# Second cross attention: two heads of attention at once, with probabilities and values split into high and low parts

## Chip, cores and metric

One core of a Trainium2 chip runs the whole program. The metric is the device time of one execution in microseconds (us).

## The reference, cut to what matters

The input is x of 8 batches of 256 rows by 256 columns, with a context of 64 rows for each batch. Two gated layers follow each other: a cross attention, a self attention with a mixture of experts, a second cross attention, a feed-forward block. The change lies in the second cross attention. Of each batch it computes, with 16 query heads of width 128 and 4 key/value heads (4 query heads share one):

```
q = rope(rms_norm(h @ wq));  k = rope(rms_norm(h @ wk));  v = h @ wv
kc = rms_norm(ctx @ wk_ctx); vc = ctx @ wv_ctx
p = softmax(q @ [kc, k].T / sqrt(128) + causal mask on the k part)   # 64 + 256 keys
x = x + tanh(g_xattn) * ((p @ [vc, v]) @ wo)
```

All of it is asked for in float32.

## The kernel before

The second cross attention is `cross_attention_1`. It walks over 32 items, NI = 4 groups x 8 batches. Item i is key/value head g = i // 8 of batch i % 8 with its four query heads h = 0 to 3. Rows are tiled in T = 2 tiles of 128. Each engine runs an order of its own that is written out by hand for one item, and engines meet only at counting semaphores. In an item's body j = i + 1 and k = i + 2 are the items of which earlier steps are already done: projections for k, transposes and first scores for j. The steps, by engine:

- TensorE (`pe`): `proj_kv`, `proj_q` (into the two banks of pA), `q_tr`, `k_tr`, `p_tr` (transposes of queries, keys and probabilities, into the two banks of pT in turn), `scores` (pS, two banks), `attend` (probabilities times values, into the one bank pO), `out_proj` (pF). Projections and `out_proj` go through `three` (L458 to L462), three matmuls of fp32r operands (high x high, high x low, low x high). `scores` and `attend` are plain float32 matmuls; the profile shows each as two instructions.
- ScalarE (`act`): `take_kv` (squares of k, copy of v), `squares` (of q), `exp`, `normalise` (the scaling by 1/sum, two instructions), the copies out of pT (`q_ev`, `k_ev`, `p_ev`), `o_ev` (the high part of pO), `w_high`.
- VectorE (`dve`): `soft` (mask and maximum, from pS), `recip`, `take_q` (two products of rope, from pA), `rotate_k`, `o_low` (the low part of pO, pO minus the high part), `add_out` (L1555, into the residual).
- GpSimd (`pool`): sums of rope, inverse norms, `context_values` (values of the context, laid on the upper or the lower half of the partitions), `context_keys`, `w_low`.

`attend(i, h)` of one head waits for the copy of the transposed probabilities (`te`) and, as pO has one bank, for `o_low` of the head before (`ot`):

```
e.matmul(pO[:, 0:S], V[:, i % 3, 0, :], PT[:, h % 2, P:P + S], start=True, stop=False)
e.matmul(pO[:, P:S], V[:, i % 3, 1, :], PT[:, h % 2, P + S:2 * P + S], start=False, stop=False)
for t in range(T):
    ins = e.matmul(pO[:, t * P:(t + 1) * P], VS[:, i % 2, t, :], PT[:, h % 2, 0:P],
                   start=False, stop=(t == 1))
```

Of the kernel before, what the change touches and what calls it, by code (L numbers as in the profile page):

```python
# [24 lines left out]
P = 128  # L25
# [42 lines left out]
def build(nc, d, out, spill, stop=99):  # L68
    ctx = ExitStack()
    with ctx:  # L70
# [1109 lines left out]
        def cross_attention_1(scope, KT, VC, w_here, cw_here, w_next, cw_next):  # L1180
# [24 lines left out]
            V = sb(name + "_V", [P, 3, T, HD], F32, scope)  # L1205
            VS = sb(name + "_VS", [P, 2, T, HD], F32, scope)
# [5 lines left out]
            PT = sb(name + "_PT", [P, 2, 4 * P], F32, scope)  # L1212
# [4 lines left out]
                     "const", "table", "vz", "vs")  # L1217
            q = {x: sem(f"{name}_{x}") for x in names}
            raw_in = [q["raw0"], q["raw1"]]

            def at_qk(i, n):

                return n if i == 0 else NT + PER * (i - 1) + (2, 3, 5)[n]

            def at_p(i, h):
                return NT + PER * i + (h if i == NI - 1 else (0, 1, 4, 6)[h])
# [25 lines left out]
            def pe(e):  # L1252
# [27 lines left out]
                def q_tr(i, t):  # L1280
                    c = at_qk(i, t)
                    e.wait_ge(q["te"], pos(c - 1))
                    e.wait_ge(q["rope"], NT * i + 2 + t)
                    for h in range(HG):
                        ins = e.transpose(pT[:, c % 2, h * P:(h + 1) * P], QR[:, t, h * HD:(h + 1) * HD],
                                          ident[:, :])
                    ins.then_inc(q["tr"], 1)

                def k_tr(i):
                    c = at_qk(i, 2)  # L1290
                    e.wait_ge(q["te"], pos(c - 1))
# [13 lines left out]
                def p_tr(i, h):  # L1305
                    c = at_p(i, h)
                    e.wait_ge(q["pn"], HG * i + h + 1)
                    e.wait_ge(q["te"], pos(c - 1))
                    for j, b in enumerate((1, 0, 3, 2)):
                        ins = e.transpose(pT[:, c % 2, j * P:(j + 1) * P], PB[:, h, b * P:(b + 1) * P],  # L1310
                                          ident[:, :])
                    ins.then_inc(q["tr"], 1)

                def attend(i, h):
                    e.wait_ge(q["te"], at_p(i, h) + 1)
                    e.wait_ge(q["ot"], HG * i + h)
                    if h == 0:
                        e.wait_ge(q["kv"], i + 1)
                        e.wait_ge(q["vs"], i + 1)
                    e.matmul(pO[:, 0:S], V[:, i % 3, 0, :], PT[:, h % 2, P:P + S], start=True, stop=False)  # L1320
                    e.matmul(pO[:, P:S], V[:, i % 3, 1, :], PT[:, h % 2, P + S:2 * P + S], start=False, stop=False)
                    for t in range(T):
                        ins = e.matmul(pO[:, t * P:(t + 1) * P], VS[:, i % 2, t, :], PT[:, h % 2, 0:P],
                                       start=False, stop=(t == 1))
                    ins.then_inc(q["pv"], 1)

                def out_proj(i, t):
                    g = i // 8
                    e.wait_ge(q["ot"], HG * i + HG)
                    e.wait_ge(q["split"], 8 * g)  # L1330
                    e.wait_ge(q["acc"], i)
                    r = slice(t * P, (t + 1) * P)
                    for h in range(HG):
                        cc = slice(WO + h * D, WO + (h + 1) * D)
                        ins = three(e, pF[:, t * D:(t + 1) * D], OTh[:, i % 2, h, r], OTl[:, i % 2, h, r],
                                    Wh[(g + 1) % 2][:, cc], Wl[(g + 1) % 2][:, cc], h == 0, h == HG - 1)
                    if t == T - 1:
                        ins.then_inc(q["f"], 1)
# [12 lines left out]
                for i in range(NI):  # L1351
# [20 lines left out]
                    attend(i, 2)  # L1372
# [9 lines left out]
                    attend(i, 3)  # L1382
# [4 lines left out]
            def act(e):  # L1387
                def take_kv(i):
                    e.wait_ge(q["proj"], NU * i + 1)
                    e.wait_ge(q["pv"], pos(HG * (i - 2)))  # L1390
                    x = pA[:, NU * i % 2, :].rearrange("p (t a n) -> p t a n", t=T, a=2)
                    for t in range(T):
                        e.activation(sk[:, t, :], x[:, t, 0, :], ACT.Square, accum_out=ssk[:, t:t + 1])
                    e.activation(V[:, i % 3, :, :], x[:, :, 1, :], ACT.Copy).then_inc(q["kv"], 1)
# [66 lines left out]
                for i in range(NI):  # L1461
# [30 lines left out]
                    o_ev(i, 3)  # L1492
                    if two:
                        squares(k, 1)
                phase_end(e, name)

            def dve(e):
# [70 lines left out]
                for i in range(NI):  # L1568
                    j, k = i + 1, i + 2
                    one, two = j < NI, k < NI  # L1570
                    soft(i, 2)
                    recip(i, 2)
                    o_low(i, 0)
# [19 lines left out]
                    o_low(i, 3)  # L1593
# [3 lines left out]
            def pool(e):  # L1597
# [678 lines left out]
```

## Time and profile before

| | |
|---|---|
| median of 3 runs | 1992.56 us (1992.42 to 1993.39) |
| profiled execution | 1994.94 us, of which span 1993.1 us |
| TensorE busy in the span | 1786.4 us (90%) |
| ScalarE | 1305.8 us (66%) |
| VectorE | 1086.7 us (55%) |
| GpSimd | 1072.5 us (54%) |

A span runs from the first to the last instruction of the core. Busy shares are averages over stages with different limits, so they don't say what the second cross attention waits for; that is read from its own stretch, about 1262 us to 1852 us of the span. In a timeline row "x4" means that four instructions are merged; the duration then reaches from the start of the first to the end of the last. An instruction's duration includes its way through the pipeline, so the next one of the same engine starts a little before it ends. The distance from start to start is called pitch in this document.

### The profile page before, as it was taken

The page shows a single profiled execution, that of the slowest core. Times are in us where ns is not written, and L with a number is a line of the kernel's source. Part 1 is how long each engine was busy: PE and PEld are TensorE (multiplying, and loading weights), DVE is VectorE, ACT ScalarE, POOL GpSimd, SP SyncE. Part 2 cuts the span into 40 slices and gives each one's busy share as a digit, 9 for nine tenths or more (in the row PEclk, how much of TensorE's full clock was granted, in tenths as well). Part 3 has the DMA queues.
Part 4 walks back from the last instruction along what each step waited for, and adds up shares of the span by engine and source line. Part 5 has one row for each costly group of instructions (what it writes and reads, how often), then busy time and mean ns, then how long its engine had stood idle before and what let it go on. Part 6 is the DMA issues. An engine that isn't in the chain of part 4 may idle for free. (4 is left out here: it accounts for less than half of the span.)

```text
span 1993.1 us, 36721 instructions
## 1 busy us (share of the span) xinstructions
PE 1786.4 (90%) x11712; PEld 1603.9 (80%) x11712; DVE 1086.7 (55%) x3117; ACT 1305.8 (66%) x4189; POOL 1072.5 (54%) x1187
## 2 busy tenths in 40 slices
PE   3499999269999999999988985799999999999698
PEld 1388888259999999999877863688888888888598
DVE  1477777656666666666534434455555555555422
ACT  1277777158888888888723313688888888888221
POOL 1433334389988988898730103544544454453364
PEclk9699999679999999999968986899999999999799
DMA  3000001110000000000001110000000000000000
GB/s 108 22 17 17 17 23 33 45 32 17 18 22 17 15 19 17 17 17 12 12 1 32 30 41 11 16 11 11 8 11 11 8 11 14 18 14 13 4 22 22
DMA packets 28385, 40.25 MB, mean 20 GB/s; under 512 B 4770, under 2 KB 18338, under 8 KB 27940
## 3 DMA queue, kind: packets, MB, share of 16 engines
q1 hardware_dynamic: 28196, 37.90, 6.3%
q8 instruction: 98, 1.61, 0.3%
q14 instruction: 91, 0.75, 0.1%
HBM read 33.69 MB, written 4.19 MB: 19 GB/s over the span
## 5 line engine op out<-in xcount | busy, mean ns | idle before, releaser
L460 PE MATMUL pA<-Wh,XTh 128*128 128x512 f32 (+1 forms) x512 | 222.6, 435 | 8.4 <-DVE x_tk L1524 3.8
L1163 POOL TENSOR_TENSOR f_sw<-f_sw,f_sin 128x512 f32<-128x512 f32 x128 | 183.6, 1434 | 38.7 <-ACT f_sw L969 38.7
L462 PE MATMUL pA<-Wh,XTl 128*128 128x512 f32 (+1 forms) x512 | 190.1, 371 | 0.0
L461 PE MATMUL pA<-Wl,XTh 128*128 128x512 f32 (+1 forms) x512 | 189.7, 370 | 0.0
L969 ACT ACTIVATE f_sw<-pA 64x512 f32<-64x512 f32 x256 | 151.8, 593 | 36.6 <-PE pA L875 32.8
L873 PE MATMUL pA<-XTh,Wh 128*128 128x256 f32 x512 | 163.7, 320 | 8.4 <-POOLq L116 6.2
L1166 POOL TENSOR_TENSOR f_sw<-f_sw,f_RB 128x512 f32<-128x512 f32 x128 | 165.1, 1290 | 10.0
L455 POOL TENSOR_TENSOR Wl<-RAW,Wh 128x256 fp32r<-128x256 f32 (+3 forms) x64 | 60.9, 952 | 175.0 <-ACT Wh L448 175.0
L1427 ACT ACTIVATE x_P<-x_P,x_nm 128x192 f32<-128x192 f32 (+1 forms) x256 | 128.0, 506 | 33.7 <-DVE x_nm L1536 33.7
L875 PE MATMUL pA<-XTh,Wl 128*128 128x256 f32 x512 | 145.9, 285 | 0.0
L874 PE MATMUL pA<-XTl,Wh 128*128 128x256 f32 x512 | 145.9, 285 | 0.0
L1631 POOL TENSOR_TENSOR x_QR<-x_QR,x_t 128x512 f32<-128x512 f32 x64 | 82.1, 1283 | 99.4 <-DVE x_QR L1513 99.4
L990 ACT ACTIVATE f_P<-f_P,f_nm 128x128 f32<-128x128 f32 (+1 forms) x256 | 114.1, 447 | 16.6 <-DVE f_nm L1076 16.5
L460 PEld LDWEIGHTS pA<-Wh,XTh 128*128 128x128 f32 x512 | 98.5, 192 | 29.3 <-DVE x_tk L1524 4.3
L1435 ACT ACTIVATE x_P<-x_P,x_rs 128x192 f32<-128x192 f32 (+1 forms) x256 | 116.3, 508 | 8.4 <-DVE x_rs L1544 8.4
L299 PE MATMUL pT<-ident,n_xn 128*128 128x128 f32 x160 | 44.1, 432 | 84.3 <-DVE n_xn L260 83.9
L1536 DVE CUSTOM_DVE_ANT_0 x_P<-pS,x_mask,x_nrq 128x192 f32<-128x192 f32 (+1 forms) x256 | 113.6, 481 | 3.5 <-PE pS L1302 2.7
L461 PEld LDWEIGHTS pA<-Wl,XTh 128*128 128x128 f32 x512 | 98.8, 193 | 18.7
L462 PEld LDWEIGHTS pA<-Wh,XTl 128*128 128x128 f32 x512 | 98.7, 193 | 17.0
L873 PEld LDWEIGHTS pA<-XTh,Wh 128*128 128x128 f32 x512 | 98.8, 193 | 11.4 <-POOLq L116 6.6
L299 PEld LDWEIGHTS pT<-ident,n_xn 128*128 128x128 f32 x160 | 29.9, 224 | 97.0 <-issue 51.5
L1076 DVE CUSTOM_DVE_ANT_0 f_P<-pS,f_mask 128x128 f32<-128x128 f32 (+1 forms) x256 | 80.8, 353 | 45.7 <-PE pS L882 45.6
(245 smaller groups left out, 6276.8 us busy)
## 6 DMA issues: line engine op xcount, KB each, us to landing
RAW<-in_w_f SPq DMA_DIRECT2D x32, 256.0 KB, 2.7
RAW<-in_w_x SPq DMA_DIRECT2D x32, 160.0 KB, 2.2
RAW<-in_w_x SPq DMA_DIRECT2D x32, 128.0 KB, 2.0
RAW<-in_w_ff SPq DMA_DIRECT2D x8, 288.0 KB, 2.8
R<-in_x SPq DMA_DIRECT2D x4, 512.0 KB, 5.8
x_spill<-R SPq DMA_DIRECT2D x1, 2048.0 KB, 7.5
RAW<-in_w_moe SPq DMA_DIRECT2D x8, 256.0 KB, 2.6
moe_xs<-x_spill SPq DMA_DIRECT2D x8, 256.0 KB, 3.0
```

The lines of the kernel that those rows point to most:

```text
L460: e.matmul(o, ah, bh, start=first, stop=False)
L461: e.matmul(o, ah, bl, start=False, stop=False)
L462: return e.matmul(o, al, bh, start=False, stop=last)
L873: e.matmul(o, Wh[g % 2][:, w], xh, start=(k == 0), stop=False)
L874: e.matmul(o, Wh[g % 2][:, w], xl, start=False, stop=False)
L875: ins = e.matmul(o, Wl[g % 2][:, w], xh, start=False, stop=(k == KD - 1))
L969: ins = e.activation(sw[dst, n, :, :], pA[src, n % 2, :].rearrange("p (a n) -> p a n", a=2), ACT.Copy)
L990: ins = e.activation(x, x, ACT.Exp, scale=-1.0, bias=nm[:, h, t:t + 1], accum_out=sm[:, h, t:t + 1])
L1163: e.tensor_tensor(y, y, bc(sind[:, :], 1, 2), ALU.mult).then_inc(q["swm"], 1)
L1166: e.tensor_tensor(y, y, RB[:, g % 2, 2 * n:2 * n + 2, :], ALU.add).then_inc(q["swb"], 1)
L1427: ins = e.activation(x, x, ACT.Exp, scale=-1.0, bias=nm[:, h, t:t + 1], accum_out=sm[:, h, t:t + 1])
L1435: ins = e.activation(x, x, ACT.Copy, scale=rs[:, h, t:t + 1])
```

## The change

`attend` takes two heads at a time: `attend(i, 0)` for heads 0 and 1, `attend(i, 1)` for heads 2 and 3, each over the whole bank pO (512 columns). It goes through `three`, with probabilities PTh/PTl and values Vh/Vl (own) and VSh/VSl (context) in fp32r. VectorE makes the low parts: `p_low` once a head from pT, `v_low` once an item from pA. GpSimd splits the context's values in `context_values`. A bank of pT that holds probabilities is free only when `p_low` is done (`bank_free`, `pl`). `o_ev` and `o_low` run twice an item over 512 columns instead of four times over 256. The orders of TensorE, ScalarE and VectorE are written anew.

```diff
@@ -1202,28 +1202,49 @@
...
-V = sb(name + "_V", [P, 3, T, HD], F32, scope)
-VS = sb(name + "_VS", [P, 2, T, HD], F32, scope)
+Vh = sb(name + "_Vh", [P, 3, T, HD], F32R, scope)
+Vl = sb(name + "_Vl", [P, 3, T, HD], F32R, scope)
+vu = sb(name + "_vu", [P, T, HD], F32, scope)
...
-PT = sb(name + "_PT", [P, 2, 4 * P], F32, scope)
+used = 8 * cw_here
+PTh, PTl = (w[0][:, used:used + 8 * P].rearrange("p (j h n) -> p j h n", j=4, h=2) for w in (Wh, Wl))
+VSh, VSl = (w[0][:, used + 8 * P:used + 12 * P].rearrange("p (u t n) -> p u t n", u=2, t=T)
+            for w in (Wh, Wl))
 OTh = sb(name + "_OTh", [P, 2, HG, S], F32R, scope)
 OTl = sb(name + "_OTl", [P, 2, HG, S], F32R, scope)
...
+turns = [("q", 0, 0), ("q", 0, 1), ("q", 0, 2)]
+for i in range(NI):
+    j = [i + 1] * (i + 1 < NI)
+    turns += [("p", i, 0), ("p", i, 1)] + [("q", x, n) for x in j for n in (0, 1)] + [("p", i, 2)]
+    turns += [("q", x, 2) for x in j] + [("p", i, 3)]
+place = {x: c for c, x in enumerate(turns)}
...
+def bank_free(e, c):
+
+
+    if c >= 2:
+        x = turns[c - 2]
+        if x[0] == "p":
+            e.wait_ge(q["pl"], HG * x[1] + x[2] + 1)
+        else:
+            e.wait_ge(q["te"], c - 1)
...
     def q_tr(i, t):
         c = at_qk(i, t)
-        e.wait_ge(q["te"], pos(c - 1))
+        bank_free(e, c)
...
@@ -1305,28 +1326,31 @@
...
-    def attend(i, h):
-        e.wait_ge(q["te"], at_p(i, h) + 1)
-        e.wait_ge(q["ot"], HG * i + h)
-        if h == 0:
+    def attend(i, w):
+        e.wait_ge(q["pl"], HG * i + 2 * w + 2)
+        e.wait_ge(q["ot"], 2 * i + w)
+        if w == 0:
             e.wait_ge(q["kv"], i + 1)
+            e.wait_ge(q["tk"], i + 1)
             e.wait_ge(q["vs"], i + 1)
-        e.matmul(pO[:, 0:S], V[:, i % 3, 0, :], PT[:, h % 2, P:P + S], start=True, stop=False)
-        e.matmul(pO[:, P:S], V[:, i % 3, 1, :], PT[:, h % 2, P + S:2 * P + S], start=False, stop=False)
-        for t in range(T):
-            ins = e.matmul(pO[:, t * P:(t + 1) * P], VS[:, i % 2, t, :], PT[:, h % 2, 0:P],
-                           start=False, stop=(t == 1))
+        v, c = i % 3, i % 2
+        three(e, pO[:, :], Vh[:, v, 0, :], Vl[:, v, 0, :], PTh[:, 1:3, :, :], PTl[:, 1:3, :, :], True, False)
+        three(e, pO[:, S:2 * S], Vh[:, v, 1, :], Vl[:, v, 1, :], PTh[:, 3, :, :], PTl[:, 3, :, :],
+              False, False)
+        for t in range(T):
+            ins = three(e, pO[:, t * S:(t + 1) * S], VSh[:, c, t, :], VSl[:, c, t, :],
+                        PTh[:, 0, :, :], PTl[:, 0, :, :], False, t == T - 1)
         ins.then_inc(q["pv"], 1)

     def out_proj(i, t):
         g = i // 8
-        e.wait_ge(q["ot"], HG * i + HG)
+        e.wait_ge(q["ot"], 2 * i + 2)
         e.wait_ge(q["split"], 8 * g)
         e.wait_ge(q["acc"], i)
...
@@ -1355,21 +1379,20 @@
         scores(i, 2)
         if two:
             proj_kv(k)
-        attend(i, 0)
         p_tr(i, 1)
         scores(i, 3)
         if one:
             q_tr(j, 0)
-            q_tr(j, 1)
         if i:
             out_proj(i - 1, 0)
-        attend(i, 1)
+        if one:
+            q_tr(j, 1)
+        attend(i, 0)
         p_tr(i, 2)
         if one:
             k_tr(j)
         if i:
             out_proj(i - 1, 1)
-        attend(i, 2)
         if one:
             scores(j, 0)
         if two:
@@ -1379,7 +1402,7 @@
             scores(j, 1)
         if two:
             proj_q(k, 1)
-        attend(i, 3)
+        attend(i, 1)
     for t in range(T):
         out_proj(NI - 1, t)
     phase_end(e, name)
...
@@ -1417,8 +1440,9 @@
     def p_ev(i, h):
         c = at_p(i, h)
         e.wait_ge(q["tr"], c + 1)
-        e.wait_ge(q["pv"], pos(HG * i + h - 1))
-        e.activation(PT[:, h % 2, :], pT[:, c % 2, :], ACT.Copy).then_inc(q["te"], 1)
+        e.wait_ge(q["pv"], 2 * i + h // 2)
+        e.activation(PTh[:, :, h % 2, :], pT[:, c % 2, :].rearrange("p (j n) -> p j n", j=4), ACT.Copy
+                     ).then_inc(q["te"], 1)
...
-    def o_ev(i, h):
-        e.wait_ge(q["pv"], HG * i + h + 1)
+    def o_ev(i, w):
+        e.wait_ge(q["pv"], 2 * i + w + 1)
         e.wait_ge(q["f"], pos(i - 1))
-        e.activation(OTh[:, i % 2, h, :], pO[:, 0:S], ACT.Copy).then_inc(q["oth"], 1)
+        e.activation(OTh[:, i % 2, 2 * w:2 * w + 2, :].rearrange("p h (t n) -> p t h n", t=T),
+                     pO[:, :].rearrange("p (t h n) -> p t h n", t=T, h=2), ACT.Copy
+                     ).then_inc(q["oth"], 1)
...
@@ -1466,32 +1492,30 @@
         exp(i, 2)
         if two:
             take_kv(k)
-        o_ev(i, 0)
         p_ev(i, 1)
         normalise(i, 2)
         if one:
             q_ev(j, 0)
+        exp(i, 3)
+        if one:
             q_ev(j, 1)
-        exp(i, 3)
-        o_ev(i, 1)
+        o_ev(i, 0)
         p_ev(i, 2)
         if one:
             k_ev(j)
         normalise(i, 3)
-        o_ev(i, 2)
         w_high(i)
         if one:
             exp(j, 0)
+            normalise(j, 0)
         p_ev(i, 3)
-        if one:
-            normalise(j, 0)
         if two:
             squares(k, 0)
         if one:
             exp(j, 1)
-        o_ev(i, 3)
         if two:
             squares(k, 1)
+        o_ev(i, 1)
...
@@ -1512,7 +1536,13 @@
...
+    def v_low(i):
+        e.wait_ge(q["kv"], i + 1)
+        x = pA[:, NU * i % 2, :].rearrange("p (t a n) -> p t a n", t=T, a=2)
+        e.tensor_tensor(Vl[:, i % 3, :, :], x[:, :, 1, :], Vh[:, i % 3, :, :].bitcast(F32), ALU.subtract)
+
     def rotate_k(i):
+        v_low(i)
         e.wait_ge(q["rk"], i + 1)
         if i >= 2:
...
@@ -1543,9 +1573,18 @@
...
+    def p_low(i, h):
+        c = at_p(i, h)
+        e.wait_ge(q["te"], c + 1)
+        e.tensor_tensor(PTl[:, :, h % 2, :], pT[:, c % 2, :].rearrange("p (j n) -> p j n", j=4),
+                        PTh[:, :, h % 2, :].bitcast(F32), ALU.subtract).then_inc(q["pl"], 1)
+
+    def o_low(i, w):
+        e.wait_ge(q["oth"], 2 * i + w + 1)
+        two_heads = slice(2 * w, 2 * w + 2)
+        e.tensor_tensor(OTl[:, i % 2, two_heads, :].rearrange("p h (t n) -> p t h n", t=T),
+                        pO[:, :].rearrange("p (t h n) -> p t h n", t=T, h=2),
+                        OTh[:, i % 2, two_heads, :].bitcast(F32).rearrange("p h (t n) -> p t h n", t=T),
                         ALU.subtract).then_inc(q["ot"], 1)
...
@@ -1569,28 +1608,30 @@
         j, k = i + 1, i + 2
         one, two = j < NI, k < NI
         soft(i, 2)
+        p_low(i, 0)
         recip(i, 2)
-        o_low(i, 0)
+        p_low(i, 1)
         soft(i, 3)
         if two:
             rotate_k(k)
         recip(i, 3)
-        o_low(i, 1)
+        o_low(i, 0)
         if i:
             add_out(i - 1)
-        o_low(i, 2)
+        p_low(i, 2)
         if one:
             soft(j, 0)
+            recip(j, 0)
         if two:
             take_q(k, 0)
-        if one:
-            recip(j, 0)
+        p_low(i, 3)
+        if one:
             soft(j, 1)
         if two:
             take_q(k, 1)
         if one:
             recip(j, 1)
-        o_low(i, 3)
+        o_low(i, 1)
...
@@ -1603,11 +1644,17 @@
...
     def context_values(i):
         g = i // 8
-        e.wait_ge(q["pv"], pos(HG * (i - 1)))
-        for t in range(T):
-            ins = e.tensor_scalar(VS[:, i % 2, t, :], VC[:, i % 8, g * HD:(g + 1) * HD],
-                                  half[:, t:t + 1], None, ALU.mult)
-        ins.then_inc(q["vs"], 1)
+        e.wait_ge(q["pv"], pos(2 * (i - 1)))
+        e.wait_ge(q["vs"], i)
+        for t in range(T):
+            ins = e.tensor_scalar(vu[:, t, :], VC[:, i % 8, g * HD:(g + 1) * HD], half[:, t:t + 1], None,
+                                  ALU.mult)
+        ins.then_inc(q["vu"], 1)
+        e.wait_ge(q["vu"], i + 1)
+        e.tensor_copy(VSh[:, i % 2], vu[:, :, :]).then_inc(q["vh"], 1)
+        e.wait_ge(q["vh"], i + 1)
+        e.tensor_tensor(VSl[:, i % 2], vu[:, :, :], VSh[:, i % 2].bitcast(F32), ALU.subtract
+                        ).then_inc(q["vs"], 1)
```

## Rows read from the trace of the kernel before

**Rows 1.** Windows; us, then busy us of each engine (instructions), granted clock, DMA.
```profile
1280.00:1840.00 560.00, 551.51 (x3709) 497.04 (x3710) 304.97 (x1008) 469.75 (x1734) 263.85 (x357) 1.00 0.04 12
1818.00:1852.00 34.00, 28.97 (x209) 25.96 (x207) 12.96 (x45) 23.75 (x75) 7.41 (x8) 1.00 0.00 1
```

**Rows 2.** Timeline of TensorE in one item: start us, duration us, line, tiles.
```profile
1568.17 0.66 PE L1285 MATMUL pT<-ident,x_QR 128*128 128x128 f32 x4 [0.20 <-ACT x_PT L1421]
...
1568.90 0.29 PE L462 MATMUL pF<-Wh,x_OTl 128*128 128x256 f32 x1
...
1570.09 0.59 PE L1320 MATMUL pO<-x_PT,x_V 128*128 128x256 f32 x2
...
1571.19 0.60 PE L1310 MATMUL pT<-ident,x_P 128*128 128x128 f32 x4
...
1573.27 0.59 PE L1320 MATMUL pO<-x_PT,x_V 128*128 128x256 f32 x2
...
1578.16 0.39 PE L461 MATMUL pA<-Wl,XTh 128*128 128x512 f32 x1
...
1579.32 0.59 PE L1320 MATMUL pO<-x_PT,x_V 128*128 128x256 f32 x2
```

**Rows 3.** Timeline of ScalarE in the same item, same columns.
```profile
1566.48 0.27 ACT L1393 ACTIVATE x_sk<-pA 128x128 f32<-128x128 f32 x1
...
1567.25 0.38 ACT L1441 ACTIVATE x_OTh<-pO 128x256 fp32r<-128x256 f32 x1
...
1576.36 0.46 ACT L1427 ACTIVATE x_P<-x_P,x_nm 128x192 f32<-128x192 f32 x1 [1.06 <-DVE x_nm L1536]
...
1577.27 0.19 ACT L1427 ACTIVATION_READ_ACCUMULATOR x_P<-x_P,x_nm 128x1 f32 x1
1577.36 0.58 ACT L1421 ACTIVATE x_PT<-pT 128x512 f32<-128x512 f32 x1
1578.22 0.91 ACT L1435 ACTIVATE x_P<-x_P,x_rs 128x192 f32<-128x192 f32 x2 [0.28 <-DVE x_rs L1544]
1579.03 0.26 ACT L1401 ACTIVATE pA<-pA 128x128 f32<-128x128 f32 x1
...
1579.88 0.26 ACT L1401 ACTIVATE pA<-pA 128x128 f32<-128x128 f32 x1
```

**Rows 4.** Timeline of VectorE in the same item, same columns.
```profile
1568.01 0.41 DVE L1536 CUSTOM_DVE_ANT_0 x_P<-pS,x_mask,x_nrq 128x192 f32<-128x192 f32 x1
...
1568.81 0.08 DVE L1536 DVE_READ_ACCUMULATOR2_ANT x_nm<- 128x1 f32 x1
1568.81 0.35 DVE L1522 SCALAR_TENSOR_TENSOR x_KR<-pA,x_ssk,x_cosk 128x128 f32<-128x128 f32 x1
...
1573.47 0.75 DVE L1555 SCALAR_TENSOR_TENSOR R<-pF,tanhg,R 128x512 f32<-128x512 f32 x1 [1.24 <-PE pF L462]
...
1576.83 0.69 DVE L1510 TENSOR_TENSOR x_t<-pA,x_sin 128x512 f32<-128x512 f32 x1 [0.50 <-PE pA L462]
...
1578.03 0.15 DVE L1544 RECIPROCAL x_rs<-x_sm 128x2 f32<-128x2 f32 x1
```

**Rows 5.** Line L266, a norm stage: durations in ns, least, median, most.
```profile
L266 DVE TENSOR_TENSOR XTl<-pT,XTh x24: 683/686/692, 67.9 to 1872.5; 128x512 fp32r<-128x512 f32 x24
```

**Rows 6.** Groups of the stage by line: busy us, mean ns of one.
```profile
L1626 POOL TENSOR_TENSOR x_KR<-x_KR,x_tk 128x256 f32<-128x256 f32 x31 | 22.6, 729 | 6.9 <-DVE x_tk L1524 3.2
```

**Rows 7.** Timeline of TensorE: items 0, 1 and 30.
```profile
1265.39 0.66 PE L1310 MATMUL pT<-ident,x_P 128*128 128x128 f32 x4 [1.94 <-ACT x_P L1435]
...
1271.21 1.19 PE L1320 MATMUL pO<-x_PT,x_V 128*128 128x256 f32 x2 [2.86 <-POOL x_VS L1608]
...
1287.37 0.60 PE L1310 MATMUL pT<-ident,x_P 128*128 128x128 f32 x4
...
1818.52 0.60 PE L1310 MATMUL pT<-ident,x_P 128*128 128x128 f32 x4
```

**Rows 8.** Line L1555, the residual add of each item: first and last start.
```profile
L1555 DVE SCALAR_TENSOR_TENSOR R<-pF,tanhg,R x32: 750/751/752, 1298.7 to 1851.6; 128x512 f32<-128x512 f32 x32
```

More of the change, by code:

```diff
@@ L1216, in cross_attention_1 @@
                      "rqb", "rq", "tr", "te", "sc", "sct", "ex", "rs", "pn", "pv", "oth", "ot", "f", "acc",
-                     "const", "table", "vz", "vs")
+                     "const", "table", "vz", "vs", "vu", "vh", "pl")
             q = {x: sem(f"{name}_{x}") for x in names}
             raw_in = [q["raw0"], q["raw1"]]
+            turns = [("q", 0, 0), ("q", 0, 1), ("q", 0, 2)]
[4 more added lines that the diff above has]
+            place = {x: c for c, x in enumerate(turns)}
             def at_qk(i, n):
-                return n if i == 0 else NT + PER * (i - 1) + (2, 3, 5)[n]
+                return place["q", i, n]
             def at_p(i, h):
-                return NT + PER * i + (h if i == NI - 1 else (0, 1, 4, 6)[h])
+                return place["p", i, h]
+            def bank_free(e, c):
[5 more added lines that the diff above has]
+                        e.wait_ge(q["te"], c - 1)
             def heads(x, swap=False):
@@ L1290, in k_tr @@
                     c = at_qk(i, 2)
-                    e.wait_ge(q["te"], pos(c - 1))
+                    bank_free(e, c)
                     e.wait_ge(q["rope"], NT * i + 1)
@@ L1307, in p_tr @@
                     e.wait_ge(q["pn"], HG * i + h + 1)
-                    e.wait_ge(q["te"], pos(c - 1))
+                    bank_free(e, c)
                     for j, b in enumerate((1, 0, 3, 2)):
@@ L1389, in take_kv @@
                     e.wait_ge(q["proj"], NU * i + 1)
-                    e.wait_ge(q["pv"], pos(HG * (i - 2)))
+                    e.wait_ge(q["pv"], pos(2 * (i - 2)))
                     x = pA[:, NU * i % 2, :].rearrange("p (t a n) -> p t a n", t=T, a=2)
@@ L1393, in take_kv @@
                         e.activation(sk[:, t, :], x[:, t, 0, :], ACT.Square, accum_out=ssk[:, t:t + 1])
-                    e.activation(V[:, i % 3, :, :], x[:, :, 1, :], ACT.Copy).then_inc(q["kv"], 1)
+                    e.activation(Vh[:, i % 3, :, :], x[:, :, 1, :], ACT.Copy).then_inc(q["kv"], 1)
                 def squares(i, t):
@@ L1544, in recip @@
                     e.reciprocal(rs[:, h, :], sm[:, h, :]).then_inc(q["rs"], 1)
-                def o_low(i, h):
-                    e.wait_ge(q["oth"], HG * i + h + 1)
-                    e.tensor_tensor(OTl[:, i % 2, h, :], pO[:, 0:S], OTh[:, i % 2, h, :].bitcast(F32),
+                def p_low(i, h):
[9 more added lines that the diff above has]
+                                    OTh[:, i % 2, two_heads, :].bitcast(F32).rearrange("p h (t n) -> p t h n", t=T),
                                     ALU.subtract).then_inc(q["ot"], 1)
```

## The prediction

> **What bounds the kernel now.** I read first the windows over the stretch of the second cross attention. From 1280 to 1840 us TensorE is busy for 551.51 of 560 us (98.5%) at the full granted clock (1.00, the 2.4 GHz level), ScalarE for 469.75 (84%), VectorE for 304.97 (54%), GpSimd for 263.85 (47%) [rows 1]. So one item after another is set by TensorE's work. The length of an item comes from the first transpose of probabilities (L1310) of item 1, at 1287.37, and of item 30, at 1818.52 [rows 7]: 531.15 us over 29 items, 18.32 us each, of which 1.5% or 0.28 us is idle and 18.04 us work. One of its waits is the second `q_tr`, 0.20 us, for the copy of probabilities out of pT [rows 2]. Then I read the timelines of one item for each engine, because the change touches all their orders: they give the price and the pitch of each step [rows 2 to 4].
>
> **TensorE's share of the change.** A head of `attend` now takes from 1570.09 to 1571.19, 1.10 us [rows 2], so four heads 4.40. The new one for two heads is three matmuls of 512 columns and nine of 256 (three for V's second half, six for the context's). A 512 in fp32r has a pitch of (1579.32 - 1578.16)/5 = 0.232 us, a 256 one of (1570.09 - 1568.90)/10 = 0.119 us [rows 2]. That makes 0.70 + 1.07 = 1.77 us for two heads, 3.54 an item, 0.86 less than now. TensorE would have 17.18 us of work an item.
>
> **The work that is added elsewhere.** `p_low` is a subtraction of 512 columns from PSUM with an fp32r output. L266 is the same instruction in another stage and takes 0.68 to 0.69 us [rows 5]; next to another such instruction the pitch is (1578.03 - 1576.83)/2 = 0.60 [rows 4]. Four of them add 2.4 us an item to VectorE, `v_low` less than one more (0 to 0.6), and `o_low`, twice at 0.60 instead of four shorter ones, at most 1.2. VectorE has 54% of 18.32, 10.0 us, now and would have up to 14.2 of about 18: as a load it is no bound. ScalarE keeps its 15.4 us: two copies of 512 for four of 256, no more than now. GpSimd adds a copy and a subtraction of 256 columns to `context_values`. The subtraction is like L1626, 0.73 us [rows 6]; the copy I bound by nothing and 0.73. At most 1.5 us on 8.6 of 18.3 us, and what it makes is wanted an item later, so it is hidden, except in item 0 (below). No transfer changes.
>
> **Why the load isn't the answer.** The new orders tie the engines in a ring. `attend(i, 0)` needs `p_low(i, 1)`; `p_low(i, 2)` stands behind `add_out(i - 1)`, which waits for `out_proj(i - 1, 1)`, which stands behind `attend(i, 0)` on TensorE. ScalarE now has `normalise(j, 0)` right behind `exp(j, 0)`, so it waits there for VectorE's `recip(j, 0)`, and `p_ev(i, 3)` stands behind both. `p_low(i, 3)` waits for that copy, `soft(j, 1)` and `take_q(k, 1)` stand behind `p_low(i, 3)`, `squares(k, 1)` waits for `take_q(k, 1)`, and `o_ev(i, 1)`, which was ahead of `squares(k, 1)`, is now last on ScalarE, behind it. `o_low(i, 1)` waits for `o_ev(i, 1)`, and the next item's `soft` of head 2 stands behind `o_low(i, 1)`. So the ring closes once an item. Round it, in us, a step's pitch where the next stands behind it on the same engine, its end plus the hand-off where another engine takes over:
>
> 1. `o_ev` of the item before 0.60 (`p_ev`, of the same size, takes 0.58), hand-off 0.04; `o_low` 0.60; `soft(i, 2)` (1568.89 - 1568.01) 0.88 + 0.04 [rows 3, 4]: 2.16.
> 2. `exp(i, 2)` 1.00, `take_kv` 0.77, `p_ev(i, 1)` 0.58 + 0.04 [rows 3]: 2.39, together 4.55.
> 3. `p_low(i, 1)` 0.69 [rows 5] + 0.04 to TensorE: 5.28.
> 4. `q_tr(j, 1)` (1568.90 less two pitches of 256, less 1568.17) 0.49, `attend(i, 0)` 1.77: 7.54.
> 5. `p_tr`, `k_tr`, `out_proj(i - 1, 1)`, from 1571.19 to 1573.27, and 0.20 to `add_out` [rows 2, 4]: 9.82.
> 6. `add_out` 0.67 (0.75 less the overlap of 0.08), `p_low(i, 2)` 0.60, `soft(j, 0)` 0.92: 12.01.
> 7. `exp(j, 0)` to the end of its sum (1576.36 to 1577.46) 1.10 + 0.04, `recip` to the start of `normalise` (1578.03 to 1578.22) 0.19, `normalise` (1578.22 to 1579.03) 0.81, `p_ev(i, 3)` 0.62 [rows 3, 4]: 14.77.
> 8. `p_low(i, 3)` 0.60, `soft(j, 1)` (1568.01 to 1568.81) 0.80, `take_q(k, 1)` 1.20 + 0.08 + 0.04: 17.49.
> 9. `squares(k, 1)`, four of (1579.88 - 1579.03)/3 = 0.283 [rows 3], 1.13: 18.62.
>
> I also followed the steps beside the ring with the same prices: TensorE reaches `p_tr(i, 1)` some 0.5 us before `normalise(i, 1)` is done, comes to `q_tr(j, 1)` 0.1 to 0.2 us before `p_low(i, 1)`, and to `attend(i, 1)` 0.9 us before `p_low(i, 3)`. These waits go into the 18.62 - 17.18 = 1.44 us that TensorE idles per item. The hand-off of 0.04 is read where ScalarE was waiting for VectorE: `recip` ends at 1578.18, `normalise` starts at 1578.22 [rows 3, 4].
>
> The page "Advanced Engine Details and Errata" of the Trainium skill (section Miscellaneous Facts, Network/Comms) gives 50 to 100 ns for reading a semaphore from a sequencer. By that figure as the price of each of the ring's ten hand-offs the ring would be 18.7 to 19.2 us instead of 18.62, 3 to 17 us more in all; the row above shows 0.04, so I don't take it.
>
> **The sum.** Items 1 to 29: 29 x (18.62 - 18.32) = +8.8 us. Item 0 takes 1287.37 - 1265.39 = 21.98 us now. In it TensorE idles 2.86 us at `attend(0, 0)` until the context's values come, and then runs at half its clock (two instructions of L1320 take 1.19 us against 0.59) [rows 2, 7]. After the change, `p_tr`, `scores` and the two `q_tr` go ahead of `attend(0, 0)`, which starts when the split values are there, 1.2 to 1.5 us later than now, at about 1272.6. From there to the end of the item the ring's steps give some 10.4 us: item 0 takes 17.6, -4.3 us. If the clock falls as before it is nearly 0. The last two items have no projections; now they take from 1818.52 to 1852.35 [rows 7, 8], 33.8 us. Item 30 walked without `take_kv`, `take_q` and `squares` comes to 18.4, item 31, where each head's copy, low part, attend and output follow each other with nothing beside them, to 17.8: +2.4 us (bounds +0.5 and +3.5). In all +8.8 - 4.3 + 2.4 = +6.9 us. The profiled execution (span 1993.1, time 1994.94) is 2.4 us above the median of the runs; its 1994.94 would become 2001.8, and the median of 1992.56 becomes 1999.5.
>
> **Bounds.** With every hand-off at nothing the ring is 18.2 us; with each full duration (0.69) for the 0.60 of low parts in it, 18.9. 29 items make that -3.5 to +17 us instead of +8.8. With the bounds of item 0 and the tail that is 1983 to 2017.
>
> **Rivals.**
> - *TensorE stays the bound (faster).* The waits overlap with work better than my ring says, and the item becomes 17.18 us of work plus the 0.28 idle of now, 17.46. Then 29 x 0.86 = 24.9, and 1992.6 - 24.9 - 1.9 gives 1966. For it: 98.5% busy TensorE, 16% idle ScalarE, 46% idle VectorE. Against: the ring would have to be 1.1 us shorter than I sum it, which is more than all its hand-offs. It decides once the ring is under 17.46. 12%. The page "FP8 and Floating Point Precision" (section Matmul Precision) of the Trainium skill states four passes for float32; as column passes two heads would go from 5120 to 3840. That is the rule by which this change gains; the rows give 2.20 to 1.77 us.
> - *No change that can be told.* The ring comes out between 18.2 and 18.45, and the item is as long as now: 1989 to 1996, about 1993. For it: my sum is only 0.30 us above today's item. 25%.
> - *The clock falls.* If TensorE's new pauses (0.5 and 0.9 us in an item) brought the half clock for a few us in each item, as the 2.86 us pause in item 0 does now [rows 7], work would be stretched by 2 to 3 us and cost 1 to 2 us an item beyond the idle time: 2030 to 2055. Against: from 1818 to 1852 TensorE is 15% idle at a granted clock of 1.00 [rows 1]. 5%.
> - *The ring as summed (my forecast).* 58%, with 1995 to 2010 as its own range.
>
> **Numbers.** I predict 1999.5. The range 1984 to 2010 holds my case and that of no change; it leaves out the faster rival (12%), the fallen clock (5%) and little of the tails. 0.2% or 4 us is about what a measurement of this kernel can tell from no change. Slower by more than that: my case less the part of it under 1996.5, 0.51, and the fallen clock, 0.05, so 0.56. Within it: most of the second rival and that part of mine, 0.27. Faster: the first rival and a ring under 18.1, 0.17.
>
> **What the profile after would show.** Right: L461/L462 of pO with pitch 0.119 and 0.232; 18.4 to 18.8 us from one L1310 of head 0 to the next; TensorE near 92% busy; `p_low` at 0.69 us; ScalarE idle before `normalise` of head 0 for VectorE's reciprocal; the copy of pO starting behind `squares`; TensorE waiting on `p_low` before `attend(i, 1)`. Wrong: a period under 18.2 with TensorE at 97% or more, a granted clock under 1.00, `p_low` far from 0.69, or item 0 still over 20 us.

## The result and the profile after

The changed kernel takes 2004.04 us (median of 5 runs, 2000.03 to 2006.59), the kernel before beside it 1993.39 us (1992.42 to 1996.10). The ratio is 1.0049, with a 95% interval of 1.0033 to 1.0065: slower, by 10.65 us in the medians. The profiled execution took 2005.44 us, with a span of 2003.6 us against 1993.1.

Windows over the stage, and over its last two items; columns as in [rows 1]:

```profile
1280.00:1840.00 560.00, 525.19 (x3403) 456.74 (x3402) 366.33 (x1078) 463.77 (x1647) 294.54 (x416) 1.00 0.04 12
1820.00:1862.00 42.00, 31.11 (x200) 26.68 (x199) 20.47 (x57) 25.48 (x77) 9.80 (x11) 0.96 0.00 1
```

TensorE is busy for 525.19 of 560 us where it was 551.51 [rows 1], at the same granted clock of 1.00. VectorE rose from 304.97 to 366.33, ScalarE fell a little. So TensorE got the time back and waits it away. The timeline of TensorE in one item shows where (in brackets: idle before, and what ended it):

```profile
1560.60 0.50 PE L460 MATMUL pO<-Wh,x_Vh 128*128 128x512 f32 x1 [0.78 <-DVE Wl L1579]
...
1565.62 0.66 PE L1331 MATMUL pT<-ident,x_P 128*128 128x128 f32 x4 [0.24 <-ACT x_P L1459]
...
1568.99 0.66 PE L1306 MATMUL pT<-ident,x_QR 128*128 128x128 f32 x4
1569.40 0.48 PE L460 MATMUL pO<-Wh,x_Vh 128*128 128x512 f32 x1
...
1571.26 0.60 PE L1331 MATMUL pT<-ident,x_P 128*128 128x128 f32 x4
...
1579.22 0.50 PE L460 MATMUL pO<-Wh,x_Vh 128*128 128x512 f32 x1 [0.78 <-DVE Wl L1579]
...
1581.10 0.60 PE L1331 MATMUL pT<-ident,x_P 128*128 128x128 f32 x4
```

An item is 1579.22 - 1560.60 = 18.62 us. The fp32r matmuls of `attend` take 1571.26 - 1569.40 = 1.86 us for two heads. From the first of them, behind the transposes, to the second it is 0.31 us (1569.40 to 1569.71), where the pitch is 0.23; the prediction had these 0.08 us in the term of `q_tr`. TensorE waits 0.78 us for the low part of the probabilities (L1579, `p_low`, whose output lies in tile Wl) before `attend(i, 1)`, and 0.24 us for ScalarE's `normalise` before `p_tr(i, 1)`.

VectorE in the same item. L1585 is `o_low`, L1579 `p_low`, L1542 `v_low`, L1574 `recip`:

```profile
1564.32 0.69 DVE L1585 TENSOR_TENSOR x_OTl<-pO,x_OTh 128x512 fp32r<-128x512 f32 x1 [1.64 <-ACT x_OTh L1465]
...
1568.24 0.69 DVE L1579 TENSOR_TENSOR Wl<-pT,Wh 128x512 fp32r<-128x512 f32 x1 [1.10 <-ACT Wh L1444]
...
1569.65 0.42 DVE L1542 TENSOR_TENSOR x_Vl<-pA,x_Vh 128x256 fp32r<-128x256 f32 x1
...
1573.53 0.75 DVE L1594 SCALAR_TENSOR_TENSOR R<-pF,tanhg,R 128x512 f32<-128x512 f32 x1 [0.76 <-PE pF L462]
1574.20 0.68 DVE L1579 TENSOR_TENSOR Wl<-pT,Wh 128x512 fp32r<-128x512 f32 x1
...
1576.85 0.17 DVE L1574 RECIPROCAL x_rs<-x_sm 128x2 f32<-128x2 f32 x1 [1.16 <-ACT x_P L1451]
...
1578.47 0.69 DVE L1579 TENSOR_TENSOR Wl<-pT,Wh 128x512 fp32r<-128x512 f32 x1 [0.25 <-ACT Wh L1444]
```

`p_low` takes 0.68 to 0.69 us. VectorE is idle for 1.64 us before `o_low` until the copy of pO is there, and for 1.16 us before the reciprocal of head 0. ScalarE shows the other side. L1424 is `squares`, L1465 `o_ev`, L1459 `normalise`, L1444 `p_ev`:

```profile
1563.42 0.26 ACT L1424 ACTIVATE pA<-pA 128x128 f32<-128x128 f32 x1
...
1563.70 0.58 ACT L1465 ACTIVATE x_OTh<-pO 128x512 fp32r<-128x512 f32 x1
...
1577.05 0.91 ACT L1459 ACTIVATE x_P<-x_P,x_rs 128x192 f32<-128x192 f32 x2 [0.23 <-DVE x_rs L1574]
1577.86 0.58 ACT L1444 ACTIVATE Wh<-pT 128x512 fp32r<-128x512 f32 x1
...
1582.32 0.58 ACT L1465 ACTIVATE x_OTh<-pO 128x512 fp32r<-128x512 f32 x1
```

The copy of pO starts at 1563.70, right behind the last of the squares, though the last matmul of `attend` had started before 1562.48. And `normalise` of head 0 waits for the reciprocal (0.23 us, [idle before]) and holds up `p_ev` of head 3. These are the ring's places.

The first and last items: TensorE's first transpose of items 0, 1, 30 and 31 (L1331), and the second `attend` of item 30; in the kernel before these are in [rows 7, 8]:

```profile
1265.19 0.66 PE L1331 MATMUL pT<-ident,x_P 128*128 128x128 f32 x4 [1.91 <-ACT x_P L1459]
...
1283.23 0.60 PE L1331 MATMUL pT<-ident,x_P 128*128 128x128 f32 x4
...
1823.12 0.60 PE L1331 MATMUL pT<-ident,x_P 128*128 128x128 f32 x4
...
1839.62 0.50 PE L460 MATMUL pO<-Wh,x_Vh 128*128 128x512 f32 x1 [2.69 <-DVE Wl L1579]
...
1842.64 1.02 PE L1331 MATMUL pT<-ident,x_P 128*128 128x128 f32 x4
```

The residual adds (L1594), as the group of that line:

```profile
L1594 DVE SCALAR_TENSOR_TENSOR R<-pF,tanhg,R x32: 750/751/752, 1294.3 to 1860.5; 128x512 f32<-128x512 f32 x32
```

By these rows the span's 10.5 us come from: the stage begins 0.20 us earlier; item 0 takes 18.04 us instead of 21.98, -3.94; items 1 to 29 take (1823.12 - 1283.23)/29 = 18.617 us instead of 18.316, +8.73; items 30 and 31 take 38.13 instead of 33.83, +4.30; all that follows takes 142.35 instead of 140.75, +1.60. The last is outside the change, whose edits all lie in the second cross attention. Of the feed-forward block's first matmuls, those of 256 columns take 0.41 us each at the half clock (1.2 GHz) until the clock rises. The kernel before comes first, then the changed one:

```profile
1873.27 0.58 PE L1968 MATMUL pA<-XTh,Wh 128*128 128x256 f32 x1 [1.46 <-DVEq L116]
...
1877.92 0.32 PE L1968 MATMUL pA<-XTh,Wh 128*128 128x256 f32 x1
```

```profile
1882.07 0.58 PE L2015 MATMUL pA<-XTh,Wh 128*128 128x256 f32 x1 [1.46 <-DVEq L116]
...
1887.14 0.41 PE L2017 MATMUL pA<-XTh,Wl 128*128 128x256 f32 x1
```

The clock rises 4.65 us after the first matmul in the one, and has not risen after 5.07 us in the other. The block's second group of matmuls starts 6.27 us after the first in the kernel before (1879.54) and 7.12 us after it in the changed one (1889.19). That is 0.85 of the 1.60 us; the rest lies further on and is not traced.

### The profile page after: what moved, and what is told of

Its sections match the earlier page's. It is cut to its first block and busy times, and to the rows that moved or that the text cites. A ratio compares the mean times of both kernels' runs of the same rounds, so it can differ in the third digit from the quotient of the medians.

```text
span 2003.6 us, 36210 instructions
## 1 busy us (share of the span) xinstructions
PE 1769.7 (88%) x11456; PEld 1571.4 (78%) x11456; DVE 1157.6 (58%) x3213; ACT 1308.2 (65%) x4125; POOL 1105.6 (55%) x1251
## 5 line engine op out<-in xcount | busy, mean ns | idle before, releaser
L1459 ACT ACTIVATE x_P<-x_P,x_rs 128x192 f32<-128x192 f32 (+1 forms) x256 | 116.5, 510 | 7.2 <-DVE x_rs L1574 7.2
L461 PEld LDWEIGHTS pA<-Wl,XTh 128*128 128x128 f32 x512 | 99.0, 193 | 18.6
L1579 DVE TENSOR_TENSOR Wl<-pT,Wh 128x512 fp32r<-128x512 f32 x128 | 88.0, 688 | 43.0 <-ACT Wh L1444 42.8
```

What stands on the lines that cost most here:

```text
L461: e.matmul(o, ah, bl, start=False, stop=False)
L1459: ins = e.activation(x, x, ACT.Copy, scale=rs[:, h, t:t + 1])
```

## The experiments

All are made from the changed kernel. Each was timed in turns with the kernel before. Runs of one kernel spread by up to 8.5 us, so the length of an item is the sharper measure. It is taken from two rows of the residual add, L1594 or the line it has in the run, some 25 items apart, both in items that have all their steps (the last ones lack projections and are shorter). In the changed kernel:

```profile
1331.51 0.75 DVE L1594 SCALAR_TENSOR_TENSOR R<-pF,tanhg,R 128x512 f32<-128x512 f32 x1 [0.75 <-PE pF L462]
...
1796.93 0.75 DVE L1594 SCALAR_TENSOR_TENSOR R<-pF,tanhg,R 128x512 f32<-128x512 f32 x1 [0.76 <-PE pF L462]
```

That is 465.42/25 = 18.617 us an item.

### The same work off TensorE, once on the ring and once beside it

```diff
+                    def product(o, ah, al, bh, bl, first, last):
+                        if w == 0:          # 1 in the other kernel
+                            return e.matmul(o, ah, bh, start=first, stop=last)
+                        return three(e, o, ah, al, bh, bl, first, last)
+
-                    three(e, pO[:, :], Vh[:, v, 0, :], Vl[:, v, 0, :], ...     # cut here
+                    product(pO[:, :], Vh[:, v, 0, :], Vl[:, v, 0, :], ...      # the other calls likewise
```

> The changed kernel, but attend(i, 0) alone makes only the product of the high parts (4 matmuls instead of 12, so the low parts of heads 0 and 1 are left out). It takes 1.18 us off TensorE in each item, on the ring: attend(i, 0) 0.59 instead of 1.77 us. Ring theory: the item becomes 18.62 - 1.18 = 17.44 us, in all about -34 us, some 1969. If TensorE's work were the bound: the same -34. If VectorE's added load or the clock were the cause: less than 10 us. Told apart from TensorE's work only beside the run that takes the same work off attend(i, 1).

> The same with attend(i, 1): only the product of the high parts for heads 2 and 3 (their low parts left out). TensorE has 1.18 us less work in each item here too, but attend(i, 1) is not on the ring: its end is followed by the copy of pO, which ScalarE reaches only behind squares(k, 1), 1.1 us or more later. Ring theory: item of 18.62 as before, 0 to -2 us in all, about 2002. TensorE's work as the bound: -34 us, about 1970.

Measured for `attend(i, 0)`: 2000.86 us against 1994.33 of the kernel before, ratio 1.0032 (1.0021 to 1.0043). The residual adds, and a row of TensorE:

```profile
1331.51 0.75 DVE L1599 SCALAR_TENSOR_TENSOR R<-pF,tanhg,R 128x512 f32<-128x512 f32 x1 [0.75 <-PE pF L462]
...
1809.48 0.75 DVE L1599 SCALAR_TENSOR_TENSOR R<-pF,tanhg,R 128x512 f32<-128x512 f32 x1 [0.75 <-PE pF L462]
...
1568.59 0.44 PE L1315 MATMUL pT<-ident,x_KR 128*128 128x128 f32 x2 [0.73 <-ACT x_qT L1436]
```

477.97/26 = 18.383 us an item: 0.23 less, not 1.18. This was a miss, and the last row shows where the rest went. `k_tr` (L1315) now waits 0.73 us for the copy of the second half of the queries, `q_ev(j, 1)` (L1436), which stands behind `exp(i, 3)` on ScalarE. The ring over `attend(i, 0)` had a second path beside it, only some 0.2 us shorter.

Measured for `attend(i, 1)`: 2005.47 us, ratio 1.0061 (1.0046 to 1.0076). The residual adds:

```profile
1331.94 0.75 DVE L1599 SCALAR_TENSOR_TENSOR R<-pF,tanhg,R 128x512 f32<-128x512 f32 x1 [0.75 <-PE pF L462]
...
1797.36 0.75 DVE L1599 SCALAR_TENSOR_TENSOR R<-pF,tanhg,R 128x512 f32<-128x512 f32 x1 [0.75 <-PE pF L462]
```

From the waits between 1300 and 1800 us, TensorE's for `normalise` (total us, times, longest):

```profile
PE pT L1331 <- ACT x_P L1464: 38.5, 27, 1.4
```

465.42/25 = 18.617 us an item, the same as with all the matmuls. `attend(i, 1)` took 0.69 us (1579.64 to 1580.33) instead of 1.88, and the 1.19 us became wait: 1.4 us before `p_tr(i, 1)` instead of 0.24. TensorE's work is not what sets the item.

### The same VectorE instruction, once on the ring and once where VectorE waits

```diff
+            junk = sb(name + "_junk", [P, 4 * P], F32, scope)
...
                     p_low(i, 3)
+                    e.tensor_tensor(junk[:, :], mask[:, :], mask[:, :], ALU.add)
                     if one:
                         soft(j, 1)
```

and in the other kernel the same line between `recip(j, 1)` and `o_low(i, 1)`.

> The changed kernel with one more VectorE instruction an item (mask + mask into a tile of its own, 512 columns, about 0.69 us long with a pitch of 0.60) between p_low(i, 3) and soft(j, 1), on the ring. Ring theory: 18.62 + 0.60 = 19.22 us an item, +17 to +20 us, about 2022. VectorE's load as the cause: the same as in the run with the instruction elsewhere. TensorE as the bound: no change.

> The same added instruction, but between recip(j, 1) and o_low(i, 1), where VectorE waits 1.64 us for the copy of pO. Ring theory: no change, 18.62 us an item, within 2 us of the changed kernel, about 2004. VectorE's load as the cause: +17 to +20 us, as with the instruction on the ring.

Measured on the ring: 2035.05 us, ratio 1.0206 (1.0190 to 1.0221). The residual adds; then GpSimd's sum of rope, the added instruction and the one behind it:

```profile
1336.56 0.75 DVE L1595 SCALAR_TENSOR_TENSOR R<-pF,tanhg,R 128x512 f32<-128x512 f32 x1 [0.75 <-PE pF L462]
...
1806.16 0.75 DVE L1595 SCALAR_TENSOR_TENSOR R<-pF,tanhg,R 128x512 f32<-128x512 f32 x1 [0.75 <-PE pF L462]
...
1576.12 1.26 POOL L1680 TENSOR_TENSOR x_QR<-x_QR,x_t 128x512 f32<-128x512 f32 x1 [3.38 <-DVE x_QR L1538]
...
1576.90 1.03 DVE L1629 TENSOR_TENSOR x_junk<-x_mask 128x512 f32<-128x512 f32 x1
1577.86 0.41 DVE L1567 CUSTOM_DVE_ANT_0 x_P<-pS,x_mask,x_nrq 128x192 f32<-128x192 f32 x1
```

469.60/24 = 19.567 us an item, 0.95 more, where 0.60 was expected. The instruction took 1.03 us instead of 0.67 in the next run and its pitch was 1577.86 - 1576.90 = 0.96. The ring carried exactly the pitch; the price of the instruction was wrong.

Measured beside the ring: 2007.30 us, ratio 1.0066 (1.0050 to 1.0083). The same rows; the added instruction starts first here, and GpSimd's takes 1.77 us instead of 1.26:

```profile
1332.91 0.75 DVE L1595 SCALAR_TENSOR_TENSOR R<-pF,tanhg,R 128x512 f32<-128x512 f32 x1 [0.75 <-PE pF L462]
...
1798.34 0.75 DVE L1595 SCALAR_TENSOR_TENSOR R<-pF,tanhg,R 128x512 f32<-128x512 f32 x1 [0.75 <-PE pF L462]
...
1564.00 0.67 DVE L1635 TENSOR_TENSOR x_junk<-x_mask 128x512 f32<-128x512 f32 x1
1565.72 0.69 DVE L1586 TENSOR_TENSOR x_OTl<-pO,x_OTh 128x512 fp32r<-128x512 f32 x1 [1.05 <-ACT x_OTh L1466]
...
1564.04 1.77 POOL L1680 TENSOR_TENSOR x_QR<-x_QR,x_t 128x512 f32<-128x512 f32 x1 [1.69 <-DVE x_QR L1538]
```

465.43/25 = 18.617 us an item, unchanged: VectorE's idle time before `o_low` took it up. The load of VectorE is not the cause.

### One part of the new order undone

```diff
                     if one:
                         exp(j, 0)
-                        normalise(j, 0)
                     p_ev(i, 3)
+                    if one:
+                        normalise(j, 0)
...
                         soft(j, 0)
-                        recip(j, 0)
                     if two:
                         take_q(k, 0)
+                    if one:
+                        recip(j, 0)
                     p_low(i, 3)
```

> The changed kernel with one part of its new orders undone: normalise(j, 0) again behind p_ev(i, 3) on ScalarE, recip(j, 0) again behind take_q(k, 0) on VectorE. It takes the wait for the reciprocal and the 0.81 us of normalise out of the ring, and take_q(k, 0) then covers exp(j, 0). Followed step by step: p_low(i, 3) starts 1.1 us earlier behind soft(j, 0), the item becomes about 17.55 us, -31 us in all, about 1973. If the loss came from the added low parts as such (VectorE's load): no change.

Measured: 1972.29 us against 1993.88 of the kernel before, ratio 0.9888 (0.9873 to 0.9903). The residual adds:

```profile
1330.20 0.75 DVE L1595 SCALAR_TENSOR_TENSOR R<-pF,tanhg,R 128x512 f32<-128x512 f32 x1 [0.76 <-PE pF L462]
...
1786.40 0.75 DVE L1595 SCALAR_TENSOR_TENSOR R<-pF,tanhg,R 128x512 f32<-128x512 f32 x1 [0.76 <-PE pF L462]
```

456.20/26 = 17.546 us an item, as followed (17.55). All the loss of an item, and 0.77 us more, hung on the place of one reciprocal and one scaling.

### The copy of pO ahead of the squares

```diff
                         exp(j, 1)
+                    o_ev(i, 1)
                     if two:
                         squares(k, 1)
-                    o_ev(i, 1)
```

> The changed kernel with o_ev(i, 1) ahead of squares(k, 1) on ScalarE, as it was before the change. The ring loses squares' 1.13 us there, but ScalarE still reaches normalise(i, 1) no earlier, so the path over p_tr(i, 1), scores(i, 3), q_tr(j, 0) and out_proj(i - 1, 0) takes over 0.2 us below: item 18.45, about -5 us, 1999. If only the ring counted: item 17.5, -33 us.

Measured: 2003.33 us, ratio 1.0048 (1.0031 to 1.0065). The residual adds, and TensorE's `p_tr(i, 1)` and `q_tr(j, 1)`:

```profile
1335.28 0.75 DVE L1594 SCALAR_TENSOR_TENSOR R<-pF,tanhg,R 128x512 f32<-128x512 f32 x1 [0.75 <-PE pF L462]
...
1798.34 0.75 DVE L1594 SCALAR_TENSOR_TENSOR R<-pF,tanhg,R 128x512 f32<-128x512 f32 x1 [0.76 <-PE pF L462]
...
1568.36 0.66 PE L1331 MATMUL pT<-ident,x_P 128*128 128x128 f32 x4 [0.36 <-ACT x_P L1459]
...
1571.58 0.60 PE L1306 MATMUL pT<-ident,x_QR 128*128 128x128 f32 x4
```

463.06/25 = 18.522 us an item, 0.095 less (0.17 expected). `q_tr(j, 1)` no longer waits; `p_tr(i, 1)` waits 0.36 us for `normalise`. That fits the path behind it being the longest now, as expected; no run shortens that path by itself to show it. Over 29 items 0.095 us make 2.8 us, which the run times can't show: the median is 0.7 us under 2004.04, and its four runs lie between 1999.64 and 2007.00. The profiled one is the slowest of them and reached the stage's first transpose 4 us later than the changed kernel (1269.24 against 1265.19), outside the change.

### Both paths over the first two heads shortened

```diff
                         q_ev(j, 0)
-                    exp(i, 3)
-                    if one:
                         q_ev(j, 1)
+                    exp(i, 3)
                     o_ev(i, 0)
```

together with the high parts alone in `attend(i, 0)`.

> As the run with only the high parts in attend(i, 0) (low parts of heads 0 and 1 left out), and q_ev(j, 1) ahead of exp(i, 3) on ScalarE. That run gained 0.24 us an item instead of 1.18, as k_tr then waited for q_ev(j, 1). With this second path shortened too, the 1.18 us must come out: item about 17.5 us, about -32 us against the changed kernel, 1972. If something else held the item at 18.4, it stays at 18.4, 2000.

Measured: 1974.78 us, ratio 0.9894 (0.9875 to 0.9913). The residual adds:

```profile
1344.45 0.74 DVE L1598 SCALAR_TENSOR_TENSOR R<-pF,tanhg,R 128x512 f32<-128x512 f32 x1
...
1782.99 0.74 DVE L1598 SCALAR_TENSOR_TENSOR R<-pF,tanhg,R 128x512 f32<-128x512 f32 x1
```

438.54/25 = 17.542 us an item (17.5 expected). That is 0.84 us less than with the high parts alone, once the copy of the queries stands ahead of `exp(i, 3)`. It fits the second path having held that run; the copy's move by itself was not run, and it also delays `exp(i, 3)` and `o_ev(i, 0)`.

### The whole computation in another order

```diff
                     normalise(i, 1)
+                    if i and one:
+                        squares(j, 1)
                     exp(i, 2)
...
-                    if two:
-                        squares(k, 1)
                     o_ev(i, 1)
...
+                    p_low(i, 2)
                     if i:
                         add_out(i - 1)
-                    p_low(i, 2)
```

with `normalise(j, 0)` and `recip(j, 0)` placed as in the run above.

> The whole computation of the changed kernel in another order: normalise(j, 0) and recip(j, 0) back as in the first run, o_ev(i, 1) last, squares(j, 1) behind normalise(i, 1) of the next item, p_low(i, 2) ahead of add_out(i - 1). Followed step by step, only a wait of 0.3 us at q_tr(j, 1) is left beside TensorE's 17.0 to 17.2 us of work: item about 17.3 us, about 1965, 1.4% faster than the kernel before. If the split itself costs more than it gives, it is not faster than the kernel before (1994).

Measured: 1964.62 us against 1993.88, ratio 0.9848 (0.9834 to 0.9863). The residual adds, and below them the window between these two:

```profile
1328.45 0.75 DVE L1595 SCALAR_TENSOR_TENSOR R<-pF,tanhg,R 128x512 f32<-128x512 f32 x1 [0.16 <-PE pF L462]
...
1777.91 0.75 DVE L1595 SCALAR_TENSOR_TENSOR R<-pF,tanhg,R 128x512 f32<-128x512 f32 x1 [0.16 <-PE pF L462]
```

```profile
1328.45:1777.91 449.46, 445.21 (x2966) 400.15 (x2965) 321.47 (x937) 396.52 (x1432) 257.23 (x364) 1.00 0.05 13
```

449.46/26 = 17.287 us an item (17.3 expected), with TensorE busy for 99.1% of it. It beats both kernels, the one before by 1.5%: the split pays once TensorE is kept fed. The single moves of this order were not run one by one, beyond the reciprocal and the scaling above.

## Why the prediction was right, point by point

- **TensorE's work.** 1.77 us for two heads was forecast from pitches of 0.232 and 0.119 us; from its start to the next transposes 1.86 was measured. With the 0.41 of `q_tr` before it that is 2.27 for step 4 of the ring, where 2.26 stood. In the last experiment, where TensorE sets the item, it is busy for 445.21/26 = 17.12 us of it, against the 17.18 of work in the prediction. In the changed kernel it is busy for 93.8%, where 92% stood: the waits of 0.78 and 0.24 us come to less than the 1.44 us of idle time forecast, and the first matmul behind a wait takes 0.34 us to the next instead of 0.23, which counts as busy.
- **Added work.** `p_low` 0.688 us against 0.69, `v_low` 0.42 within 0 to 0.6. The loads are no bound: shown by the VectorE instruction that cost nothing beside the ring.
- **The ring.** 18.62 us was summed and 18.617 measured, and not by luck of the sum: the starts in the changed kernel's timelines give each of the nine steps within 0.02 us.

| step | from | to | summed | measured |
|---|---|---|---|---|
| 1 | copy of pO, 1563.70 | `exp(i, 2)`, 1565.85 | 2.16 | 2.15 |
| 2 | `exp(i, 2)` | `p_low(i, 1)`, 1568.24 | 2.39 | 2.39 |
| 3 | `p_low(i, 1)` | `q_tr(j, 1)`, 1568.99 | 0.73 | 0.75 |
| 4 | `q_tr(j, 1)` | `p_tr(i, 2)`, 1571.26 | 2.26 | 2.27 |
| 5 | `p_tr(i, 2)` | `add_out`, 1573.53 | 2.28 | 2.27 |
| 6 | `add_out` | `exp(j, 0)`, 1575.72 | 2.19 | 2.19 |
| 7 | `exp(j, 0)` | `p_low(i, 3)`, 1578.47 | 2.76 | 2.75 |
| 8 | `p_low(i, 3)` | `squares(k, 1)`, 1581.20 | 2.72 | 2.73 |
| 9 | `squares(k, 1)` | copy of pO, 1582.32 | 1.13 | 1.12 |

  That the time hangs on the ring is shown by experiment at two of its places: the pitch of an instruction added behind `p_low(i, 3)` came out in full (0.95 for 0.96 us), and the place of `normalise(j, 0)` and `recip(j, 0)` was worth the 1.07 us that the walk gave. The same instruction and the same TensorE work off the ring were worth nothing. That TensorE idles before `attend(i, 1)` was forecast with 0.9 us and measured with 0.78, before `p_tr(i, 1)` 0.5 against 0.24.
- **What the ring's sum did not say.** It gives the length, but not what shortening one step is worth. The prediction noted the steps beside it, TensorE's path over `p_tr(i, 1)` included, but not the path over `q_ev(j, 1)` and `k_tr`, 0.2 us shorter than the ring. Taking 1.18 us out of `attend(i, 0)` gave 0.23. The expectation of that run was wrong for this reason.
- **Item 0.** -3.94 us against the forecast -4.3, at the full clock as assumed (granted clock 1.00 from 1265 to 1283). `attend(0, 0)` started at 1272.28, where 1272.6 stood, and from there to the end of the item it took 10.95 us, where 10.4 stood.
- **The tail.** This is the term that was mis-sized: +4.30 us against +2.4, outside its upper bound of 3.5. Right behind 2.69 us of idle time before the second `attend` of item 30 TensorE's clock fell to the half (1.2 GHz) for some 3 us: the granted clock is 1.00 from 1836 to 1840, 0.63 from 1839 to 1843 and 1.00 again from 1846 on. This `attend` takes 1842.64 - 1839.62 = 3.02 us instead of the 1.88 of full clock (1579.22 to 1581.10), and the copy of pO waits for it. That is 1.14 of the 1.9 us missed, and all that item 30 takes over its forecast: 19.52 us (1823.12 to 1842.64) against 18.4. Item 31 takes 18.6 us (to 1861.25) against 17.8; its first four transposes still run at the half clock (0.85 us to the next instruction instead of 0.43), and which of its steps holds the rest is open. The prediction weighed the clock for pauses below 1 us and for item 0, and not for the last items.
- **The rest.** +1.60 us lies behind the stage and was in no term. The instructions there are the same in both kernels; 0.85 us of it come with the clock that rises later in the feed-forward block. From the end of the last residual add to the end of the span the eight experiments above took 141.8 to 144.1 us, the changed kernel 142.35 and the one profiled execution of the kernel before 140.75. Whether this term follows from the change or from the chance of single executions is not shown.
- **The rivals.** TensorE as the bound is excluded by the run with less TensorE work off the ring, no change by an item of 18.617 us instead of 18.2 to 18.45 and by the interval of the ratio, the fallen clock by the granted 1.00 from 1280 to 1840 us. A hand-off took 0.04 us from ScalarE to VectorE (`o_ev` ends at 1564.28, `o_low` starts at 1564.32) and 0.06 from VectorE to TensorE (`p_low` ends at 1579.16, the matmul starts at 1579.22). The Trainium skill's page "Advanced Engine Details and Errata" (section Miscellaneous Facts) gives 50 to 100 ns for reading a semaphore; the first of these hand-offs lies under that, the second inside it, and the ring of 18.617 us leaves no room for it as the price of all ten.
- **The bounds.** The stated 1983 to 2017 doesn't come out of the terms given with it: 1992.56 - 3.5 - 4.3 + 0.5 is 1985.3, and 1992.56 + 17 + 0 + 3.5 is 2013.1. The forecast doesn't rest on it.
- In all: forecast +6.9 us, measured +10.65, interval of the ratio +6.6 to +13 us. Of the difference the ring's 29 items have next to nothing (+8.73 for +8.8); it lies in the tail, the rest and item 0.

## What to carry to other kernels

When four engines each run a fixed order, busy shares and saved work don't give the time: write down which step waits for which, follow the loop that returns to its start one item later, and sum pitches and hand-offs round it. Then look for the second-longest path before pricing any saving: here one took over after 0.2 us, another after 0.1. A quick step that answers another engine (a reciprocal, a copy that frees a bank) should stand where its input is just ready, not right behind its source and not behind a long step that nobody waits for. In this kernel the first was worth 1.07 us an item, the second by itself 0.095.

## What the runs showed of the hardware

- A VectorE instruction with both inputs in SBUF and a GpSimd instruction delay each other. On the ring GpSimd's sum (1576.12 to 1577.38) was under way when the added instruction started at 1576.90, and that took 1.03 us instead of 0.67. Beside the ring the added instruction started first, at 1564.00, and GpSimd's sum took 1.77 us instead of 1.26. The page "SBUF — State Buffer" of the Trainium skill (section SBUF: two separate sides) states such an exclusive lock of a shared port pair for a VectorE instruction with two SBUF inputs against a GpSimd instruction that reads SBUF, and that whichever starts first keeps it. The runs agree in direction and in who waits, and nearly in size: on the ring the added instruction ended at 1577.93, 0.55 us behind GpSimd's, beside the ring GpSimd's ended at 1565.81, 1.14 us behind the added one. The low parts, with one input in PSUM, stayed at 0.68 to 0.69 us: `p_low` took 0.69 from 1578.47 in the changed kernel, while GpSimd's sum ran from 1578.30 to 1579.56.
- TensorE's granted clock stayed at 1.00 with pauses of 0.24 and 0.78 us in each item, and fell to the half right behind a pause of 2.69 us, as it did in the kernel before behind one of 2.86 us [rows 7]. A pause of 1.91 us before item 0 left it at 1.00.
